# Two token blocks of the scan output accumulated by one adding transfer per state instead of by GpSimd

## What is computed

```
dA = exp(delta[..., None] * A)                      # per channel and state
dBu = (delta * u)[..., None] * B_ssm[:, :, None, :]
h = dA_i * h + dBu_i                                # a recurrence over the 512 tokens
y = einsum('bds,bs->bd', h, c_i)                    # a sum over the 16 states
y = y + u * D_param
```

## Time and profile before

| what | value |
|---|---|
| median of 3 runs | 3334.84 us (3334.56 to 3337.2) |
| span of the profiled execution, first to last instruction | 3334.1 us |
| its own time, by the nearest thing shown (the median) | 3334.84 us, 0.7 us more than the span |
| stage of the 16 batches | about 2,780 us |
| one batch, from its first scan to the next one's | 161 us |
| mean granted TensorE clock | 0.93 of full |

### The profile page before, as it was taken

One profiled execution on the slowest core, in us unless ns is written; L12 is line 12 of the kernel. 1 busy time (PEld: TensorE's weight loads), 2 busy tenths in 40 slices (PEclk: granted clock), 3 DMA queues, 4 the chain that ended last, 5 costly groups with the idle time before them and its releaser, 6 DMA issues. The chain is left out here.

```text
span 3334.1 us, 46771 instructions
## 1 busy us (share of the span) xinstructions
PE 2825.2 (85%) x12696; PEld 1879.2 (56%) x12697; DVE 2553.8 (77%) x4108; ACT 2075.7 (62%) x3786; POOL 2588.7 (78%) x2474
## 2 busy tenths in 40 slices
PE   4686979797979797888888888889787779999998
PEld 2444555555555555555565556555545447777776
DVE  3498999999999999999999898989898842222222
ACT  3577677776767676776767676777665414444443
POOL 1399898989899898989898989898999913444443
PEclk7897989998989899999999999999998889999999
DMA  2011111111111111111011111011113213433433
GB/s 76 23 33 32 36 45 36 43 41 39 41 40 39 39 44 37 45 36 50 28 51 30 51 31 48 33 47 36 38 37 96 90 51 60 63 62 62 63 63 51
DMA packets 113899, 155.39 MB, mean 47 GB/s; under 512 B 15472, under 2 KB 73264, under 8 KB 113712
## 3 DMA queue, kind: packets, MB, share of 16 engines
q1 hardware_dynamic: 77344, 109.32, 10.6%
q0 software_dynamic: 25728, 34.75, 6.4%
q10 hardware_dynamic: 10640, 9.09, 0.8%
HBM read 107.36 MB, written 45.76 MB: 46 GB/s over the span
## 5 line engine op out<-in xcount | busy, mean ns | idle before, releaser
L872 POOL TENSOR_TENSOR dbu<-du,bbc 128x512 f32<-128x512 f32 x1024 | 1292.4, 1280 | 58.5 <-DVE h L1440 51.2
L1440 DVE TENSOR_TENSOR_SCAN h<-bank,dbu 128x512 f32<-128x512 f32 x1024 | 1224.4, 1211 | 103.9 <-POOL dbu L872 52.1
L1082 ACT ACTIVATE bank<-region,amat 128x512 f32<-128x512 f32 x1024 | 697.2, 690 | 302.4 <-DVE h L1440 295.3
L665 PE MATMUL bank<-ident,h 128*128 128x128 f32 x4096 | 633.3, 292 | 225.5 <-DVE acc L1430 198.1
L665 PEld LDWEIGHTS bank<-ident,h 128*128 128x128 f32 x4096 | 507.6, 150 | 511.5 <-DVE acc L1430 204.4
L858 POOL TENSOR_TENSOR acc<-acc,hTc 128x512 f32<-128x512 f32 x480 | 609.3, 1270 | 98.9 <-ACT hTc L1066 97.9
L1607 POOL DMA_INDIRECT out<-ye,ids x136 | 213.6, 1570 | 348.3 <-DMA out<-ye,ids 313.2
L1066 ACT ACTIVATE hTc<-bank,cT 128x512 f32<-128x512 f32 x480 | 327.4, 682 | 240.6 <-PE bank L665 236.3
L1430 DVE SCALAR_TENSOR_TENSOR acc<-bank,cT,acc 128x512 f32<-128x512 f32 x544 | 395.8, 730 | 47.6 <-PE bank L665 45.3
L619 PE MATMUL bank<-x4T,w_su 128*128 128x512 f32 (+1 forms) x768 | 391.2, 613 | 10.7 <-DVE score L1305 10.7
L1643 DVE SCALAR_TENSOR_TENSOR gg<-gt,bank 128x352 f32<-128x352 f32 x136 | 71.0, 522 | 382.9 <-ACT gt L1577 382.9
(11 more groups left out here) (204 smaller groups left out, 4357.0 us busy)
## 6 DMA issues: line engine op xcount, KB each, us to landing
bbc<-b_scratch SPq DMA_DIRECT2D x256, 256.0 KB, 3.1
xe<-slots_in SPq DMA_DIRECT2D x136, 129.0 KB
region<-in_x SPq DMA_DIRECT2D x16, 512.0 KB, 3.8
out<-x ACTq DMA_DIRECT2D x16, 512.0 KB, 3.0
region<-in_e_gu SPq DMA_DIRECT2D x8, 704.0 KB, 5.5
out<-ye,ids POOLq DMA_INDIRECT x136
slots_in<-dbu SPq DMA_DIRECT2D x16, 129.0 KB, 2.7
slots_in<-x,pos POOLq DMA_INDIRECT x128, 2.6
```

Source lines behind the costliest of these rows:

```text
L665: last = tr(scan[f"hT{s}.{t}"][:, m * P:(m + 1) * P], h[:, s % 2, m, t * P:(t + 1) * P], ident[:, :])
L872: g.tensor_tensor(dbu[:, n % 4, :], du[:, m, :], bbc[:, (b * NS + s) % NROW, :], ALU.mult).then_inc(S("dbu_ready"), 1)
L1082: f(db(n)[:, :], delta[:, 1 - par, m, :], ACT.Exp, scale=amat[:, m, s:s + 1]).then_inc(S("da_ready"), 1)
L1440: v.tensor_tensor_scan(h[:, s % 2, m, :], db(n)[:, :], dbu[:, n % 4, :], 0.0, ALU.mult, ALU.add)\
```

## The change

Blocks 2 and 3 (the list SENT) of states 0 to 13 now go the second way, in place of blocks 1 and 3 of states 0 to 14: 28 pairs of a batch in place of 30. ACT scales both into one buffer `hTc` of 128x2x512. When block 3 is scaled, POOL no longer computes: it issues one DMA that adds `hTc` to `acc[:, 2:4, :]`, 128x1024 elements, in SBUF. The buffer is single (NSENT = 1), so ACT waits for state s - 1's transfer to land before it scales block 2 of state s. DVE takes blocks 0 and 1 of every state, and all blocks of states 14 and 15: 36 additions of a batch in place of 34. The table entry `qT` goes from 62 to 61.

```diff
-POOLED = [(s, t) for s, t in ADDS if t % 2 == 1 and s < NS - 1]
+SENT, LAST_SENT, NSENT = (2, 3), NS - 2, 1
+POOLED = [(s, t) for s, t in ADDS if t in SENT and s < LAST_SENT]
...
-        hTc = sb("hTc", [P, 2, DI])
+        hTc = sb("hTc", [P, NSENT, len(SENT), DI])
...
-            xb=54, q=46, q_dve=56, qT_pe=57, qT=62, ffn_pe=(61, 63), ...
+            xb=54, q=46, q_dve=56, qT_pe=57, qT=61, ffn_pe=(61, 63), ...
...
+        def sent_added(eng, b, s):
+
+            if b * LAST_SENT + s >= 0:
+                eng.wait_ge(sent, 16 * (b * LAST_SENT + s + 1))
+
         def acc_before(eng, b, s, t):
...
             elif (s - 1, t) in POOLED:
-                done(eng, "acc_added", b, POOLED.index((s - 1, t)))
+                sent_added(eng, b, s - 1)
...
                         done(pe, "acc_ready", b)
-                        done(pe, "acc_added", b)
+                        sent_added(pe, b, LAST_SENT - 1)
...
-                def add_scaled(s, t):
-
-                    if (s, t) not in POOLED:
+                def send_scaled(s, t):
+
+                    if (s, t) not in POOLED or t != SENT[-1]:
                         return
-                    k = POOLED.index((s, t))
-                    done(pool, "scaled", b, k)
-                    acc_before(pool, b, s, t)
-                    g.tensor_tensor(acc[:, t, :], acc[:, t, :], hTc[:, k % 2, :], ALU.add).then_inc(S("acc_added"), 1)
+                    done(pool, "scaled", b, POOLED.index((s, t)))
+                    if s == 0:
+                        for block in SENT:
+                            done(pool, "acc_init", b, block)
+                    sent_added(pool, b, s - 1)
+                    g.dma_start(acc[:, SENT[0]:SENT[-1] + 1, :], hTc[:, s % NSENT, :, :], accum_op=ALU.add).then_inc(sent, 16)
...
                     scan.filled(act, f"hT{s}.{t}", b)
-                    before(act, "acc_added", b, k - 1)
-                    f(hTc[:, k % 2, :], scan[f"hT{s}.{t}"][:, :], ACT.Copy, scale=cT[:, par, t, s:s + 1]).then_inc(S("scaled"), 1)
+                    if t == SENT[0]:
+                        sent_added(act, b, s - NSENT)
+                    f(hTc[:, s % NSENT, t - SENT[0], :], scan[f"hT{s}.{t}"][:, :], ACT.Copy, scale=cT[:, par, t, s:s + 1]).then_inc(S("scaled"), 1)
```

More of the change, by code:

```diff
@@ L272, in layers @@
                    b_stored=1, cT_ready=1, da_ready=UNITS, dbu_ready=UNITS,
-                   scan_done=UNITS, acc_init=TT, acc_ready=len(KEPT), scaled=len(POOLED), acc_added=len(POOLED), y3_ready=MC,
+                   scan_done=UNITS, acc_init=TT, acc_ready=len(KEPT), scaled=len(POOLED), y3_ready=MC,
                    x3_ready=2, x4_ready=1, x4T_ready=DC, lexp_ready=1, sg1_ready=1, sg_ready=1, tag_ready=1, pos_ready=1, tok_set=1, weight_set=1,
@@ L278, in layers @@
         b_row = [sem(f"b_row{k}") for k in range(NROW)]
+        sent = sem("sent")
         dispatched = [sem(f"dispatched{w}") for w in range(2)]
@@ L315, in layers @@
             probs=(18, 21, 24, 29), probT_pe=(29, 35, 36, 38), probT=(31, 36, 38, 39), av=(41, 45), x1=(48, 52), stats2=52, rstd2=51,
-            xb=54, q=46, q_dve=56, qT_pe=57, qT=62, ffn_pe=(61, 63), ffn=(61, 63), x2=64, store=0, tags=(39, 53), q_round=55, q_nan=55,
+            xb=54, q=46, q_dve=56, qT_pe=57, qT=61, ffn_pe=(61, 63), ffn=(61, 63), x2=64, store=0, tags=(39, 53), q_round=55, q_nan=55,
             q_fin=57)
@@ L873, in scans @@
                     if n >= LAG + 2:
-                        add_scaled(*divmod(n - LAG - 2, TT))
+                        send_scaled(*divmod(n - LAG - 2, TT))
                     issue(streams, n - 3)
                 for k in range(UNITS - LAG - 2, UNITS):
-                    add_scaled(*divmod(k, TT))
+                    send_scaled(*divmod(k, TT))
                 issue(streams, END - 1)
```

## The result

The changed kernel takes 3352.96 us (median of 4 runs, 3350.76 to 3355.14) against 3336.02 us (4 runs, 3334.56 to 3337.29) for the kernel before: a ratio of 1.0046, 95% interval 1.0034 to 1.0058. It is 0.5% slower. I had forecast 3327 us, a small gain. The profiled execution's span is 3348.9 us, 14.8 more than before.

The account below looks back on a forecast made before the run. The prediction took DVE as the bound, with POOL at 92% running alongside with little harm. It summed 16 batches x (-0.8 for the batch's end + 0.3 for bank order) = -8 us, giving 3327 us, held within 3315 to 3345.

Parts of the forecast that it names:

- Parts 1 to 3: End of the batch: POOL's additions gone, DVE's two more additions, and qT one unit earlier together give -0.8 us per batch.
- The wait at scan 61: DVE's 1.03 us wait for POOL's product late in each batch; said to go, gaining 0.95 us per batch.
- the 1.81 us for state 15's transposes: DVE's wait behind scan 63 for PE's first transposes of state 15, taken to hide one extra addition.
- Part 3: qT's copy on ACT one unit earlier, some 2 us, frees PE ahead of state 14's transposes of blocks 2 and 3.
- part 2: DVE's two more additions per batch: one on the path between scans 62 and 63, +0.65 us, the other hidden.
- Part 4: PE's transposes of block 3 wait for DVE's addition of block 1 in bank 5: +0.3 us per batch, between 0 and 1.1.
- Part 5: The adding transfer and ACT's wait for it: 6.4 us to landing, just inside the shortest distances, so counted as 0.
- the prediction's last remark on part 5: DVE instructions reading two SBUF tensors stand between two batches, where no send is due; sum and chance unchanged.
- The transfer is late: Rival: ACT's scaling of block 2 waits for the landing and sets the pace; +40 us, 3375 us; chance 0.27.
- More relief: Rival: POOL's relief also removes DVE's 1.87 us wait early in each batch; 3297 us; chance 0.11.
- the wait of 1.87 us: DVE's wait early in each batch, behind POOL's small chain of norm steps; expected to stay.
- Nothing is gained: Rival: the freed wait reappears behind PE, and DVE's addition and the bank order cost +15 us; 3350 us; chance 0.12.

Follow-up runs that it names:

- 4 columns: GpSimd's additions cut to 4 of 512 columns: in the kernel before 3300.24 us; with blocks 2 and 3 of states 0 to 13 and qT=61, no transfer, 3340.47 us.
- after: The changed kernel itself, with adding transfers of blocks 2 and 3, against the kernel before: 3352.96 us, ratio 1.0046.
- Late scaling: The changed kernel with ACT's scaling of block 2 moved behind the next exponential, together with block 3: 3338.18 us, ratio 1.0004.
- single transfers: Kernel before, each GpSimd addition of blocks 1 and 3 replaced by its own adding transfer, 29 per batch: 3338.78 us; with 4 of 512 columns each, 3334.34 us.

## Why the forecast was wrong

*What bounds the kernel.* Right: DVE stayed at 92%, and POOL's relief took one of two waits per batch. Too small: of the 52 us that bounded the relief I took 0.95 us per batch, 15 us, from the timeline of one batch in the middle. With nothing else changed it is 38 us. Nearly half lies in the last two batches, which that timeline and my window of 400 to 2400 us leave out.

*The sum.* By the medians, the relief is -38 us (forecast: -15), the choice of blocks with its two more additions +40 (forecast: +15), `qT` nothing (forecast: -8), and the transfer in place of 4 columns +12.5 (forecast: 0). That is +15 us, where after and before differ by 17. So a low price for the relief hid part of too low a price for the order.

*Parts 1 to 3, the end of the batch (-0.8 per batch).* The sum came out, -0.83 in state 15, but by luck: the relief alone made state 15 1.4 us shorter (forecast: 0.95), and the additions cost 0.9 (forecast: 0.65). The wait at scan 61 is gone, and of the 1.81 us for state 15's transposes two short waits are left, 0.61 and 0.36:

```profile
1743.36 1.21 DVE L1450 TENSOR_TENSOR_SCAN h<-bank,dbu 128x512 f32<-128x512 f32 x1
...
1744.49 1.38 DVE L1440 SCALAR_TENSOR_TENSOR acc<-bank,cT,acc 128x512 f32<-128x512 f32 x2
...
1746.48 1.60 DVE L1440 SCALAR_TENSOR_TENSOR acc<-bank,cT,acc 128x512 f32<-128x512 f32 x2 [0.61 <-PE bank L672]
...
1748.44 0.75 DVE L1440 SCALAR_TENSOR_TENSOR acc<-bank,cT,acc 128x512 f32<-128x512 f32 x1 [0.36 <-PE bank L672]
```

Part 3 was worth nothing, and part 2 was mis-sized. I called one of the two additions hidden in DVE's wait, and charged 0.65 us. The two together cost 15 us in all, 0.93 per batch: with the wait mostly gone, part of the second is on the path too. A cover that the same change removes can't be counted as cover.

*Part 4, the bank order (+0.3, at most 1.1).* **This is the step that failed.** I asked only how much later PE gets bank 5. I did not ask what ACT does with bank 4, and put ACT's wait there at nothing. Block 1's scaling mostly found its transposes ready, since PE turns blocks 0 and 1 at the first unit of a state: in batches 2 to 13 it waited 36 times, 36 us in all. Block 2 is turned at the third, and ACT's scaling stands right behind it, ahead of the copies and the next exponential: 81 waits, 92 us. States 7 and 11 are 2.3 us longer per batch. Moving the scaling behind the exponential shortened these two by 2.8, and the whole by 15 us. The 15 us are a net figure, since states 9 and 13 took back what 7 and 11 gave and most of the gain lies in batches 0 to 3, where it was not followed wait by wait. Without transfers the same move was worth 13 us. Of the 40 us of the new order the two additions are 15 and this place 13; the cause of the last 12 stays open. (State 10's +0.8 goes with state 9's -0.6 and the 128x64 product.)

*Part 5, the transfer (0).* Right that its landing is hidden in the middle of the run: 4.7 us against distances from 6.5, and ACT's 33 short waits for it there hold up no exponential that a scan waits for. Wrong for its ends: all distances were read in one batch of the middle. In batch 0, which takes 150 us and not 161, four scans waited 4.2 us behind late landings, and by just as much batch 0 is longer than in the same kernel with 4 columns on GpSimd. After is 12.5 us above that kernel in all. The rest I could not trace to one wait: by state it is +0.8 in state 10 and -0.8 in state 9. It is open which part of it is POOL's 0.9 us per issue, and which the changed moments at which the 128x64 product meets GpSimd. That product is also where the prediction's last remark on part 5 went wrong: a DVE instruction with two SBUF inputs does stand beside a send, in state 9. In after it held up no send there. In most of the other kernels it was itself held up by GpSimd.

*The rivals.* "The transfer is late" is refuted for the middle of the run and true at its ends, at 8.6 us of scans' waits where the rival had 48. "More relief" is refuted in its own terms, since the wait of 1.87 us stayed, though the relief was larger than forecast. "Nothing is gained" came out, at 3350 us by its working. Its mechanism was half right (the additions). The other half that was found is ACT's order; whether the banks' order has a part in what is open was not tested.

No kernel with the whole computation beat the one before. Late scaling, at 3338.18 us, equals it.

## What to carry to other kernels

When a block moves from one consumer to another, look up on every engine what stands *behind* its new place in the queue, and whether its producer is done by then. Here ACT's scaling moved from a block long turned to one just being turned, and held an exponential and a copy that DVE needs. In this case relieving an engine that runs beside the bound was worth no more than the waits for it, the new order cost as much again, and a single step moved by one unit cost 15 us too.

Test the relief and the new order apart, with work left out, before writing the transfer. Two kernels with 4 columns (3300 and 3340 us) told more than the transfer itself. And look at the first and last batches separately: here nearly half of the relief lay in the last two, and the late landings in the first and the last two.

## What the runs showed of the hardware

- An adding transfer within SBUF lands 4.7 us after its issue for 128x1024 fp32, 3.8 us for 128x2x256, and 3.4 us for 128x512 (its median in the kernel with single transfers). GpSimd spends 0.89 us on the issue of 128 rows of 4 KB and 0.91 us (mean) on 128 rows of 16 bytes, but 1.21 us on 256 rows of 1 KB. In these kernels the issue went by rows, not by bytes.
- 173 such transfers in 2,000 us raised the DMA engines from 13% to 37%. With single transfers, where nothing else differed, leaving the data out was worth 4 us (3338.78 and 3334.34 us).
- A DVE product with two SBUF inputs lasted until GpSimd's computing instructions beside it ended: 128x64 took 0.21 to 3.80 us. The time is in the instruction's own duration, not in the idle time before it.
- An issue on GpSimd alone did not hold that product up: it ran inside one in 0.21 us.
